# One more shared-expert unit ahead of the routed slots, an earlier third gate, earlier slot loads, later word reads, and 39 slots for 40

## What is computed

```python
logits = (x @ wt.T + repeat(g @ wg.T)) / 2
scores = softmax(logits)                       # 8 experts
topk_w, topk_idx = top_k(scores, 2)            # normalised to sum 1
gp = leaky(einsum('th,ehm->etm', x, w_gate))   # h = 256, m = 128
up = einsum('th,ehm->etm', x, w_up)
y_all = einsum('etm,emh->eth', gp * up, w_down)
y = sum over the 2 chosen experts of topk_w * y_all
p = leaky(x @ sw_gate) * (x @ sw_up) @ sw_down # shared expert, width 2 x 128
out = x + relu((y + p) @ W1 + b1) @ W2 + b2
```

## Time and profile before

| | |
|---|---|
| median of 3 runs | 503.56 us (501.65 to 506.19) |
| the profiled execution, whole | 497.93 us |
| its span, first to last instruction | 496.1 us |
| mean granted TensorE clock, share of full speed | 0.966 |
| PE busy | 456.6 us, 92% |
| DVE busy | 345.8 us, 70% |
| ACT busy | 260.2 us, 52% |
| POOL busy | 274.4 us, 55% |

### The profile page before, as it was taken

How to read it: one execution, slowest core, us unless ns; L and a number is a source line. 1 busy time by engine, 2 the same in 40 slices (tenths; PEclk the granted TensorE clock), 3 DMA queues, 4 the chain that set the end, 5 groups by cost and what they waited for, 6 DMA issues and landing times.

```text
span 496.1 us, 11748 instructions
## 1 busy us (share of the span) xinstructions
PE 456.6 (92%) x4033; PEld 405.2 (82%) x4033; DVE 345.8 (70%) x875; ACT 260.2 (52%) x518; POOL 274.4 (55%) x299
## 2 busy tenths in 40 slices
PE   6797788999999999999989894999899899999996
PEld 3686677888889888888878784989897689898886
DVE  5787898888888888888888666577664635354422
ACT  4664566756656665766443313375653444444443
POOL 5779889897979799898747770000003260707000
PEclk9888999999999999999988978799999999999999
DMA  7661008347290901010103223556623120313101
GB/s 241 141 202 34 1 2 279 114 155 238 82 309 16 344 31 32 0 32 3 34 28 125 104 106 96 175 177 222 206 98 96 53 74 31 103 35 100 37 8 42
DMA packets 51663, 52.17 MB, mean 105 GB/s; under 512 B 6692, under 2 KB 49062, under 8 KB 51624
## 3 DMA queue, kind: packets, MB, share of 16 engines
q1 hardware_dynamic: 47428, 42.46, 27.0%
q0 software_dynamic: 3072, 8.39, 5.2%
q10 hardware_dynamic: 1124, 0.81, 0.6%
HBM read 22.03 MB, written 29.62 MB: 104 GB/s over the span
## 4 chain that ended last, share of the span: by engine, by line
PE 60%; DVE 14%; POOL 11%; issue 8%; ACT 4%; DMA 2%; SPq 1%; DVEq 0%; POOLq 0%; ACTq 0%
PE bank L339 9%; PE bank L340 8%; PE bank L341 8%; PE bank L344 6%; PE bank L345 5%; PE bank L1767 3%; POOL rn L616 2%; POOL sim L611 2%; PE bank L1533 2%; PE bank L1468 2%; POOL pr L596 2%; POOL wu_l L583 2%; ACT oT_h L771 2%; PE bank L1498 2%; DVE den L1109 2%
## 5 line engine op out<-in xcount | busy, mean ns | idle before, releaser
L640 POOL DMA_INDIRECT yg<-slot_y,yrow x32 | 34.3, 1071 | 126.0 <-DMA slot_y<-yb 81.1
L616 POOL TENSOR_TENSOR rn<-sc,half 128x6 f32<-128x6 f32 (+1 forms) x48 | 60.1, 1274 | 3.1 <-DVE sc L1084 2.0
L1333 DVE TENSOR_TENSOR hl<-hw,hh 128x512 fp32r<-128x512 f32 x32 | 22.2, 693 | 55.8 <-ACT hw L904 55.8
L902 ACT ACTIVATE hh<-bank,late 128x512 fp32r<-128x512 f32 x32 | 22.0, 688 | 52.2 <-PE bank L1767 42.0
L344 PE MATMUL bank<-wout_h,oT_h 128*128 128x256 f32 x128 | 33.9, 301 | 5.0 <-DVE oT_l L1095 5.0
L596 POOL TENSOR_TENSOR pr<-pe,rden 128x1024 f32<-128x1024 f32 x16 | 30.5, 1904 | 13.0 <-DVE rden L1112 12.2
L339 PE MATMUL bank<-wqkv_h,xnT_h 128*128 128x384 f32 x96 | 35.8, 372 | 1.2 <-DVE wqkv_l L932 0.6
L632 POOL DMA_INDIRECT slot_x<-xs,posi x32 | 31.1, 971 | 10.0 <-issue 9.7
L611 POOL TENSOR_TENSOR sim<-sim,mx 128x1040 f32<-128x1040 f32 x16 | 30.9, 1934 | 9.9 <-DVE mx L1073 9.8
L579 POOL TENSOR_TENSOR biasm<-bias,mneg 128x1040 f32<-128x1040 f32 x16 | 35.7, 2233 | 0.1
L1081 DVE TENSOR_REDUCE ss<-sq 128x6 f32<-128x384 f32 (+1 forms) x48 | 25.3, 527 | 12.5 <-ACT sq L756 12.4
(11 more groups left out here) (327 smaller groups left out, 1556.6 us busy)
## 6 DMA issues: line engine op xcount, KB each, us to landing
slot_x<-zrow SPq DMA_DIRECT2D x4, 4352.0 KB, 14.5
slot_y<-yb SPq DMA_DIRECT2D x20, 256.0 KB, 2.3
xq<-slot_x SPq DMA_DIRECT2D x36, 128.0 KB, 2.2
fstage<-in_f_W SPq DMA_DIRECT2D x4, 512.0 KB, 4.9
out<-p_all SPq DMA_DIRECT2D x8, 256.0 KB, 2.2
raw_out<-in_c_Wout SPq DMA_DIRECT2D x2, 512.0 KB, 8.1
xs<-in_x SPq DMA_DIRECT2D x1, 1024.0 KB, 9.1
stage<-in_m_wgate SPq DMA_DIRECT2D x8, 128.0 KB, 2.1
```

Source lines behind the costliest of these rows:

```text
L616: e.tensor_tensor(rn[:, lo:hi], sc[:, lo:hi], half[:, lo:hi], ALU.pow).then_inc(sems['rn'], 1)
L640: e.indirect_dma_start(out=yg[:, g % 2, r, t, :], out_offset=None, in_=ydram.ap()[:, :], in_offset=bass.IndirectOffsetOnAxis(ap=yrow[:, g ...
```

## The change

It has six parts.

1. `AHEAD = EARLY + 1`: unit 4's gate and up (with their ACT and DVE steps) stand before the slots; its `down(4)` stays after them. After the slots, unit 5 takes the place of unit 4 among the last slot steps. The banks of the late units swap by parity.
2. On PE `gate(2)` goes ahead of `ranks(3)`, and `up(2)` ahead of `down(0)`; `down(2)` goes between `gate(4)` and `up(4)`.
3. On ACT the four row addresses and the four `xq` loads go ahead of the two `p_all` copies of `shared_out(1)`, and behind `unit_upper(4)`.
4. On PE the five word reads go behind `down(3)`, the last work ahead of the slots.
5. On DVE `slot_rows` goes behind `unit_product(3)`, and the split of the last expert's weights (`wu_l<-stage,wu_h`) behind unit 4's steps. PE's waits for that split and for `p_all` move from ahead of the first transposes to ahead of the first gate and up products of the slots.
6. Slot 40 is left out: the last pair has one tile in place of two in every step (`in_pair`). 2 x 2048 rows over 8 experts never fill more than 39 slots.

```diff
+        MOST = SLOTS - 1
+        def in_pair(s):
+            return min(2, MOST - 2 * s)
         EARLY = 4
+        AHEAD = EARLY + 1
...
         def gate_bank(n):
-            return bank[5 - n % 2] if n < EARLY else bank[n % 2 * 4]
+            return bank[5 - n % 2] if n < AHEAD else bank[(n + 1) % 2 * 4]
...
             unit_upper(2)
             shared_out(0)
+            unit_gate(4)
             unit_upper(3)
+            unit_upper(4)
             e.wait_ge(sems['tab'], 2)
...
-            shared_out(1)
-
             e.wait_ge(sems['st_x'], 16 * 2 * NT)
             for s in range(XQ):
                 e.dma_start(xq[:, s, 1, :], xdram.ap()[bass.ds(first_rows[s], P), :]).then_inc(sems[f'ld_xq{s}'], 16)
+            shared_out(1)
...
             unit_lower(2)
-            slot_rows()
             unit_leak(3)
             unit_product(3)
+            slot_rows()
+            unit_lower(3)
+            unit_leak(4)
+            unit_product(4)
+            unit_lower(4)
             split_unit(U - 1)
-            unit_lower(3)
...
             up(1)
+            gate(2)
             ranks(3)
+            up(2)
             down(0)
-            gate(2)
-            up(2)
             gate(3)
             up(3)
             down(1)
+            gate(4)
+            down(2)
+            up(4)
+            down(3)
             e.wait_ge(sems['tab'], 1)
             words = [e.value_load(tab_w[0:1, w:w + 1], min_val=0, max_val=E ** WORD - 1) for w in range(SLOTS // WORD)]
-            down(2)
-            down(3)
...
             e.wait_ge(sems['pos'], due(NB))
-            e.wait_ge(sems['hw'], EARLY)
-            e.wait_ge(sems['p'], 2 * (EARLY // NS))
-            e.wait_ge(sems['unit'], U)
+            e.wait_ge(sems['hw'], AHEAD)
             slot_transpose(0)
             for s in range(PAIRS2):
                 if s + 1 < PAIRS2:
                     slot_transpose(s + 1)
+                if s == 0:
+                    e.wait_ge(sems['p'], 2 * (EARLY // NS))
+                    e.wait_ge(sems['unit'], U)
                 slot_gate_up(s)
...
             e.wait_ge(sems['bxl'], due(PAIRS2))
-            gate(4)
+            gate(5)
             slot_h_transpose(PAIRS2 - 1)
             slot_down_project(PAIRS2 - 2)
-            up(4)
+            up(5)
             slot_down_project(PAIRS2 - 1)
-            gate(5)
-            up(5)
             down(4)
             gate(6)
             up(6)
```

More of the change, by code:

```diff
@@ L324, in gate_bank @@
         def gate_bank(n):
-            return bank[5 - n % 2] if n < EARLY else bank[n % 2 * 4]
+            return bank[5 - n % 2] if n < AHEAD else bank[(n + 1) % 2 * 4]
         def up_bank(n):
-            return bank[6 + n % 2] if n < EARLY else bank[1 + n % 2 * 4]
+            return bank[6 + n % 2] if n < AHEAD else bank[1 + (n + 1) % 2 * 4]
         def at_tile(t3, i):
@@ L416, in load_slots @@
                 e.wait_ge(sems['bx_t'], due(s - XQ + 1))
-                for t in range(2):
+                for t in range(in_pair(s)):
                     row_j = slot_row(s, t)
@@ L849, in slot_x @@
                 e.wait_ge(sems['bgu_t'], due(s - 1))
-                e.activation(bxT_h[:, s % 2, :, :, :].rearrange('p t k m -> p (t k m)'), bank[s % 2][:, :], ACT.Copy).then_inc(sems['bxh'], 1)
+                e.activation(bxT_h[:, s % 2, 0:in_pair(s), :, :].rearrange('p t k m -> p (t k m)'), bank[s % 2][:, 0:in_pair(s) * D], ACT.Copy).then_inc(sems['bxh'], 1)
             def slot_leak(s):
@@ L854, in slot_leak @@
                 e.wait_ge(sems['ba'], due(s))
[L855 removed]
+                e.activation(bg[:, 0:in_pair(s), :], bank[2 + s % 2][:, 0:in_pair(s) * D].rearrange('p (t h m) -> p t h m', h=2, m=M)[:, :, 0, :], ACT.Copy, scale=0.01).then_inc(sems['bg'], 1)
             def slot_h(s):
@@ L859, in slot_h @@
                 e.wait_ge(sems['bdn_t'], due(s - 1))
-                e.activation(bhT_h[:, s % 2, :, :], bank[4 + s % 2][:, 0:2 * P].rearrange('p (t m) -> p t m', t=2), ACT.Copy).then_inc(sems['bhh'], 1)
+                e.activation(bhT_h[:, s % 2, 0:in_pair(s), :], bank[4 + s % 2][:, 0:in_pair(s) * P].rearrange('p (t m) -> p t m', m=P), ACT.Copy).then_inc(sems['bhh'], 1)
             def slot_y(s):
@@ L880, in _ @@
             slot_y(PAIRS2 - 1)
-            for n in range(EARLY, NU):
+            for n in range(AHEAD, NU):
                 unit_gate(n)
@@ L1664, in slot_transpose @@
             def slot_transpose(s):
-                e.wait_ge(sems[f'ld_xq{s % XQ}'], 32 * (s // XQ + 1))
+                e.wait_ge(sems[f'ld_xq{s % XQ}'], 32 * (s // XQ) + 16 * in_pair(s))
                 e.wait_ge(sems['bxl'], due(s - 1))
-                for t in range(2):
+                for t in range(in_pair(s)):
                     for k in range(KD):
```

21 lines of the change are left out of this document (11 added, 10 removed).

## The result

Before, the kernel takes 503.19 us (median of 21 runs, 498.22 to 506.19), changed 497.02 us (21 runs, 491.80 to 499.06). The ratio is 0.9933, 95% interval 0.9906 to 0.9959; it is taken over undisturbed runs alone, where the medians of all 21 give 0.988. The forecast was 499.4 us, in a range of 495.8 to 503.2. So the ratio by itself does not tell the change from none, and what the change gives is read from the traces.

What follows compares the result with a forecast made beforehand. PE's waits were taken as the bound: for DVE's chain and first loads ahead of the slots, for gathers behind. -3.1 - 1.3 - 1.8 + 2.0 = -4.2 us, from the median 503.56 to 499.4 us, range 495.8 to 503.2.

Steps and rivals of the forecast that it cites:

- The front, -3.1: Ahead of the slots: DVE's chain and the first loads come earlier, first gate product at 307.1 instead of 310.29; -3.1 us.
- the 309: Start of the slots: the prediction would be wrong if the first gate product came later than 309 us.
- full clock is what I take: PE's work behind the router wait: assumed at full clock, since `gate(2)` fills 1.4 of the 2.23 us stall.
- the 2.65 taken from SP: ACT ahead of the slots: four row address reads assumed to cost 2.65 us, as on SP.
- The copies hold the slots by half a microsecond: Start of the slots: ACT's copies, now behind the four loads, delay the slots by half a microsecond.
- The left-out slot, -1.3: The slots: one tile fewer saves 1.3 us (0 to -1.6), the stage going from 64.5 to 63.2.
- The tail, -1.8: Behind the slots: PE's work comes 4.0 us earlier, but gathers become the bound, so only -1.8 us arrives.
- T + 16.9: Behind the slots: earliest start of the last tile's transposes, counted from the last slot product's end T; before, T + 18.7.
- The clock behind the slots, +2.0: Dense layer: after a 5.5 us stall, 4.5 us run at half clock, costing +2.0 us (0 to +3.0).
- the rival that the clock stays at full: Behind the slots: no fall of the clock, total -6.2 us, 497.4 us; chance 0.22.
- The front gains little: Rival, ahead of the slots: reads or scatter's landing set the first load; front -1.0 to -1.5, total 501.3; chance 0.20.
- Slower: Rival, start of the slots: half clock outlasts it; 21 us more at half gives +5.3, 508.9 us; chance 0.06.

Runs made afterwards that it cites:

- first and second pair: Two pairs of profiles, kernel before and changed kernel, the second made later; from the ranks to the end the change gives 4.55 and 5.31 us.
- gate2_late: Changed kernel with `gate(2)` put back behind `ranks(3)`, so the router wait is empty again; 498.30 us, ratio 0.9980 to the kernel before.
- the first set: Earliest set of follow-up runs (four units ahead, 40 slots, half the gathers, filler at both stalls); the kernel before took 512.8 us in it.
- copies_first: Changed kernel with ACT's `shared_out(1)` copies ahead of the address reads and loads again; 495.51 us, ratio 0.9861 to the kernel before.
- slots40: Changed kernel with all 40 slots instead of 39; 513.78 us, ratio 1.0057 to the kernel before.
- words_early: Changed kernel with PE's five word reads ahead of `down(2)`, `up(4)` and `down(3)` again; 499.70 us, ratio 0.9964 to the kernel before.
- half_gathers: Changed kernel without group 0's second gathers, the first rows mixed twice, so another output; 508.21 us, ratio 0.9962 to the kernel before.
- warm_both: Changed kernel with unused filler transposes around the word reads and before the last two tiles' transposes; 508.55 us, 0.9872; again 495.31 us, 0.9896.
- warm_front: Changed kernel with 31 unused filler transposes between and behind the word reads only; 498.49 us, ratio 0.9876 to the kernel before.

## Why the prediction was right, point by point

**The front, -3.1.** Measured -2.7 and -3.1 (first gate product, first and second pair). By the clock of the profile the first gate product is at 312.65, later than the 309 that the prediction named as a sign of being wrong; but the ranks came 5.05 us later than before, and counted from them it is at 22.15, where 309 would be 23.55. The steps, counted from the ranks: end of `hw(1)` forecast at 3.1, measured 2.85; row table 11.65, 11.40; `hw(4)` 13.55, 13.33; first load on ACT 16.3 to 16.9, 15.88; transposes 18.75, 19.12 and 18.54; gate product 21.65, 22.15 and 21.57. The chain of DVE was read rightly, and its condition too: "full clock is what I take, since `gate(2)` fills 1.4 of the 2.23 us" is the term on which all of it stands, as `gate2_late` shows. In three profiles of the first set the front gave 0.1 to 0.8 us, with stalls that the prediction did not have and that no run explains. Two sizes were off and cancelled. The four address reads on ACT take 1.76 to 1.89 us, not the 2.65 taken from SP, and the first load takes 2.65 to 3.24 from issue to PE's start, not 2.2. **"The copies hold the slots by half a microsecond, which is the price of part 3" is wrong:** ACT waited 1.03 us for PE's eight transposes at half clock (1.94 us) with its copies done, and `copies_first` shows no price of part 3 in either direction.

**The left-out slot, -1.3.** The slot is worth 1.2, but the stage as a whole moved by 0.1 to 0.4, not from 64.5 to 63.2. The half clock at its start was taken as unchanged, and it was up to 2.6 us longer; a load came up to 1.1 us later than in the first profile of before. Both vary between executions of one kernel.

**The tail, -1.8.** Measured -2.94. The forecast's T + 16.9 for the last transposes, 0.2 of it for the shorter copy, would be T + 17.1 with 40 slots, and `slots40` has 17.09: the gathers did become the bound, at the place given. Missed is what the left-out slot does here: the first gather comes 0.63 us earlier, not 0.2, and the row of gathers is 0.6 to 0.7 shorter. The last store, of 128 KB, landed 1.7 us after its issue in both profiles of the changed kernel, and that of 256 KB 2.1 us in `before` and `slots40`; this is the other 0.4. The Trainium skill, "DMA: Bandwidth & Descriptors", anatomy of a GpSimd transfer, would have given 0.3 of that for the halved store, an estimate that was left out of the sum. The difference is near, but the page's fit is for GpSimd and this store goes by SP's queue: as a whole it gives 2.6 and 2.3 us, and the trace has 2.1 and 1.7. DVE's waits for DMA and PE's for DVE (0.48 and 1.77; "1 and 2.5") stand where they were forecast.

**The clock behind the slots, +2.0.** Measured +1.17 and +1.16, and +2.0 and +2.5 in `words_early` and `copies_first`, which have the same tail; what sets the length of the fall stayed open. All of it lies in the first group of the dense layer: the three later groups take the same time in all profiles within 0.2 us, as the prediction asked. The stretch from 393.99 to 401.99 of the changed kernel has a clock of 0.79, that is 3.4 us at half where 4.5 were taken (at the price of 0.44 that would be 1.5 us, 0.3 more than was lost); 0.62 in `copies_first`, 6.1 us. `half_gathers`, which shortens the wait, and both `warm_both`, which fill it, have no fall, and so show the cause. In all seven profiles with a wait of 1.75 to 2.11 us there, the dense layer begins at half clock (a first matmul of 0.76 or 0.77 us, where `half_gathers` has 0.47), and the rival that the clock stays at full fell. The rule of the Trainium skill, "TensorE: Matmul & The Clock Gate", "HAM oscillation", gave the right sign here, but the traces do not bear it out as the prediction put it. These waits are for DVE and ACT, not for a DMA. Behind the 2.41 us wait for a load before the change the eight transposes took 1.06 us, full clock (1.94 is half), and those of `warm_front` 1.07 us behind a wait of 2.32; in both the clock fell only afterwards. Nor did work start at half behind the 3.62 us: the clock fell about 1 us into it.

**The rivals.** "The front gains little" fell in its cause: 15.88 us to the first load, none of it the scatter's (SP's first load, which waits for the same rows, went out 14.08 us behind the ranks). "Slower" did not come: 6.2 us at half was the longest in the slots.

**The sum, -4.2,** against -4.55 and -5.31: an error of 1.1 in the tail and one of 0.8 in the clock, both on the gain's side, less 0.9 to 1.2 that the slots did not show. The mechanisms were right, but that the sum comes so near is in part luck, since three of its four terms are off by about 1 us. Not every part was tried alone: part 5 and the place of `up(2)` have no run of their own. The time of 499.4 hangs on the median of three runs as a start, 503.56; the 21 runs have 503.19.

## What to carry to other kernels

A short wait of PE is worth more than its length if the clock falls behind it: moving 1.4 us of ready work into a wait of 2.2 us gave about 3 us here, as PE's work behind it ran at full clock again and two engines that waited for it came earlier. Fill such waits with work that is needed; filler helped only where it lasted until the awaited data came. When a bound moves to a row of transfers, look at everything that the change does to their start, and set stages against stages, since spans of one kernel differ by more than such a change gives. Take more than one profile even so: in the first set the front's distance was 2 to 3 us longer with the same order of work.

## What the runs showed of the hardware

- One instruction stream, unchanged, reached the ranks at 285.45 and at 291.84 us; from 256 to 262 us the clock was 1.00 in one and 0.50 in the other.
- In the first set of runs the ranks stood near 301.5 in three of four profiles. Here rows without a releaser do stand, right behind the end of the loop, on three engines at once. DVE and PE of `slots40`:

```profile
288.92 0.42 DVE L1113 TENSOR_TENSOR xs<-bank,xs 128x256 f32<-128x256 f32 x1 [7.35 <-remote]
```

```profile
289.40 0.69 PE L1565 MATMUL bank<-ident,xs 128*128 128x128 f32 x2 [5.73 <-issue]
```

  What held them was not tried. The Trainium skill, "Runtime: NRT & Kernel Launch", "Instruction fetch mechanics", says that a taken branch breaks the sequential prefetch of instructions; no row here shows a fetch that an engine waited for.
- Eight gathers keep POOL busy for 8.2 to 8.3 us in all three profiles with 40 slots (single ones of 1.1 to 1.2 us among those of 0.95), and for 7.6 us in all with 39 that gather all rows. The cause is open. With the slot the change also drops a tile of the table `slot_y` (39 tiles of 128 rows for 40), and no run separated the two.
- A DMA on ACT's queue was issued 0.20 us after a 0.60 us copy ahead of it began (`copies_first`).
- The last store of the slots landed 2.1 us after issue with 256 KB and 1.7 us with 128 KB, on SP's queue.
